# Routing inside the expert pairs of a fused attention and experts kernel: powers made one pair ahead, another order on GpSimd and VectorE, all slots written out

## The reference

```python
# x, ctx: (16, 256, 256); 8 experts, hidden width 704, the two best experts of each token
def attention(q, c, wq, wk, wv):           # q is ctx, c is the normalized x
    Q, K, V = c @ wq, q @ wk, q @ wv
    return softmax(Q @ K.T) @ V
def experts(x, Wg, W1, W2, W3):
    scores = x @ Wg.T
    top_scores, top_idx = top_k(scores, 2)
    y[e] = (silu(x @ W1[e].T) * (x @ W2[e].T)) @ W3[e].T
    return sum(top_scores[k] * y[top_idx[k]] for k in range(2))
x = x + tanh(g_xattn) * attention(ctx, layernorm(x), wq, wk, wv)
x = x + tanh(g_ffn) * experts(layernorm(x), Wg, W1, W2, W3)
```

## Time and profile before

| what | value |
|---|---|
| runs | 657.65, 661.85, 660.46 us, median 660.46 |
| profiled execution | 661.32 us, its span 659.5 us |
| busy TensorE (matmuls) | 589.5 us, 89% |
| busy VectorE, ScalarE, GpSimd | 318.4, 329.6, 269.1 us |
| mean granted TensorE clock | 0.962 |
| chain that ended last | PE 61%, DVE 12%, ACT 10%, issue 8%, POOL 5% |

### The profile page before, as it was taken

One profiled execution on the slowest core, in us unless ns is written; L12 is line 12 of the kernel. 1 busy time (PEld: TensorE's weight loads), 2 busy tenths in 40 slices (PEclk: granted clock), 3 DMA queues, 4 the chain that ended last, 5 costly groups with the idle time before them and its releaser, 6 DMA issues.

```text
span 659.5 us, 15092 instructions
## 1 busy us (share of the span) xinstructions
PE 589.5 (89%) x4765; PEld 511.8 (78%) x4766; DVE 318.4 (48%) x860; ACT 329.6 (50%) x474; POOL 269.1 (41%) x245
## 2 busy tenths in 40 slices
PE   5898989898688967789699999799999999999995
PEld 4787878777567855678598989698989898988783
DVE  2488877797656434456333333243433343343332
ACT  3778787887734243433344444244444444444442
POOL 3155565655513655546133333223233333333322
PEclk9899999999878987899799999899999999999999
DMA  8476666855412322215232323132323232322322
GB/s 254 142 233 188 219 203 220 258 169 165 149 35 85 68 60 68 59 34 138 58 59 43 58 36 52 31 54 43 59 43 59 42 56 39 52 42 43 50 43 25
DMA packets 52372, 61.53 MB, mean 93 GB/s; under 512 B 7632, under 2 KB 46160, under 8 KB 52304
## 3 DMA queue, kind: packets, MB, share of 16 engines
q1 hardware_dynamic: 34656, 38.15, 19.2%
q0 software_dynamic: 13296, 18.23, 16.0%
q10 hardware_dynamic: 4352, 4.20, 1.8%
HBM read 36.90 MB, written 23.66 MB: 92 GB/s over the span
## 4 chain that ended last, share of the span: by engine, by line
PE 61%; DVE 12%; ACT 10%; issue 8%; POOL 5%; DMA 2%; another core or an unknown queue 1%; SPq 0%; POOLq 0%; ACTq 0%; DVEq 0%
PE psum L923 30%; PE psum L963 18%; PE psum L818 4%; PE psum L932 4%; PE psum L943 2%; DMA w_in<-in_W3T 2%; ACT w_hi L715 2%; POOL rows_by_expert L586 2%; DVE w_lo L1072 2%; ACT arena L678 2%; ACT w_hi L687 1%; ACT w_hi L691 1%; DVE w_lo L1065 1%; POOL out L623 1%; PE psum L856 1%
## 5 line engine op out<-in xcount | busy, mean ns | idle before, releaser
L623 POOL DMA_INDIRECT out<-w_in,id_s x71 | 126.8, 1786 | 249.2 <-ACT w_in L767 132.4
L923 PE MATMUL psum<-arena,w_hi 128*128 128x256 f16 x1408 | 217.3, 278 | 5.5 <-issue 4.1
L923 PEld LDWEIGHTS psum<-arena,w_hi 128*128 x1408 | 140.3, 100 | 24.7 <-issue 6.2
L923 PE MATMUL psum<-arena,w_lo 128*128 128x256 f16 x704 | 136.9, 277 | 0.0
L749 ACT ACTIVATE arena<-psum 128x1024 f16<-128x1024 f16 (+1 forms) x39 | 36.9, 947 | 95.3 <-PE psum L943 94.8
L818 PE MATMUL psum<-arena 128*128 128x256 f32 x256 | 66.3, 404 | 19.0 <-ACT arena L701 19.0
L1353 DVE SCALAR_TENSOR_TENSOR arena<-psum,h_unit,arena 128x1280 f32<-128x1280 f32 x32 | 49.6, 1550 | 63.8 <-PE psum L923 63.8
L586 POOL DMA_INDIRECT rows_by_expert<-xn2r,slot_i x64 | 66.3, 1036 | 33.8 <-issue 17.4
L923 PEld LDWEIGHTS psum<-arena,w_lo 128*128 x704 | 70.2, 100 | 9.3
L818 PEld LDWEIGHTS psum<-arena 128*128 128x128 f32 x256 | 47.9, 197 | 28.0 <-ACT arena L701 22.4
L1347 DVE SCALAR_TENSOR_TENSOR arena<-psum,h_unit,arena 64x256 f32<-64x256 f32 x32 | 15.7, 491 | 92.3 <-ACT arena L740 92.2
(11 more groups left out here) (183 smaller groups left out, 906.4 us busy)
## 6 DMA issues: line engine op xcount, KB each, us to landing
xa<-rows_by_expert SPq DMA_DIRECT2D x71, 136.0 KB
w_in<-in_W1T SPq DMA_DIRECT2D x8, 704.0 KB
w_in<-in_W3T SPq DMA_DIRECT2D x8, 640.0 KB
w_in<-in_W2T SPq DMA_DIRECT2D x8, 640.0 KB
arena<-in_ctxT SPq DMA_DIRECT2D x16, 256.0 KB
xa<-in_x SPq DMA_DIRECT2D x16, 256.0 KB, 6.0
out<-xa ACTq DMA_DIRECT2D x16, 256.0 KB
out<-w_in,id_s POOLq DMA_INDIRECT x71, 4.4
```

What stands on the lines that cost most here:

```text
L623: pool.indirect_dma_start(out=out[:, :], out_offset=bass.IndirectOffsetOnAxis(ap=id_s[:, t8:t8 + 1], axis=0), in_=y_s[:, t8 % 4, :], in_of ...
L923: ins = pe.matmul(flat_ps[:, j * N2:(j + 1) * N2], w12[w_part][:, c, bass.ds(e * (2 * H) + j * P, P)], xg_t[:, k, x_part, c, :], start=(q ...
```

## The change

- **Slots.** over_slots writes out all 39 slots; no loop and no register-valued wait is left, on GpSimd neither.
- **GpSimd.** In step i: second add of pair i-2, scatter for the batch of pair i-1, low rows for the batch of pair i, power for the batch of pair i+1, first add of pair i-1. The scatter of batch 9 and the low rows of batch 10 move from ahead of the wait for the stores to behind it.
- **VectorE.** In step i: choose (pair i-1's batch), high_rows (pair i's), mixed, weights, slots, moments of pair i+1's batch, combined, low. The units for the scales (units) are made in step 15; choose of batch 9 comes before the last low weights.
- **TensorE.** The rank product stands behind the 17 matmuls of the output. The rows of pair 0 are turned in the last step, before the values of batch 14. Pair 0 begins before the last low weights are there (it waits for them ahead of its sixth chunk), and the probabilities of batch 15 are turned after four of its chunks.
- **ScalarE.** copy_turned for pair 0 in the last step; the last high weights, silu's first call and copy_probs at the head of step 0; norm_rows ahead of copy_rows, copy_turned and high.
- **SyncE.** Pair 0's load no longer waits for the ninth low rows and the fifth even store; pair 1's does.

The diff, cut (functions that are only moved, and the tests for a written index, are left out):

```diff
...
@@ -398,24 +388,15 @@
             for u in range(n):
                 expert[u] = eng.snap(held[UNROLL - n + u], min_val=0, max_val=E - 1)
-        def over_slots(eng, step, take=lambda i, n: None, planned=lambda: None):
-
-
-            def written(a, b):
-                for i in range(a, b):
-                    step(i, i // 2, i % 4, i % UNROLL, lambda m: 0 <= m < SLOTS)
-            written(-2, 0)
-            take(0, EARLY)
-            written(0, EARLY)
-            planned()
-            with eng.Fori(0, 2) as r:
-                take(UNROLL * r + EARLY, UNROLL)
-                for u in range(UNROLL):
-                    step(UNROLL * r + EARLY + u, UNROLL // 2 * r + (EARLY + u) // 2, u % 4, u, lambda m: True)
-            take(PAIRS - UNROLL, UNROLL)
-            written(PAIRS - UNROLL, PAIRS)
-            take(PAIRS, SINGLES)
-            written(PAIRS, SLOTS + 1)
+        def over_slots(eng, step, take=lambda i, n: None):
+
+
+            for i in range(-2, SLOTS + 1):
+                if i >= 0 and i % UNROLL == 0:
+                    if i == EARLY:
+                        eng.wait_ge(s_map, 2)
+                    take(i, min(UNROLL, SLOTS - i))
+                step(i, i // 2, i % 4, i % UNROLL, lambda m: 0 <= m < SLOTS)
         block = ctx.enter_context(nc.Block())
@@ -482,8 +463,7 @@
             sp.wait_ge(s_map, 1)
             for k in range(2):
                 sp.wait_ge(s_scat[k], 16 * KT * TOP_K * ((COUNTED + 1 - k) // 2))
-                sp.wait_ge(s_x2st[k], 16 * (5 - k))
-            sp.wait_ge(s_xn2, 9)
+                sp.wait_ge(s_x2st[k], 16 * 4)
             pad_at = [sp.alloc_register(f"pad_at_{e}") for e in range(E)]
@@ -504,12 +484,15 @@
             def moe_step(i, j, k4, u, on):
                 k = k4 % 2
-                if isinstance(i, int) and i == EARLY - 2:
+                if i == -1:
+                    sp.wait_ge(s_xn2, 9)
+                    sp.wait_ge(s_x2st[0], 16 * 5)
+                if i == EARLY - 2:
                     pads()
                     all_rows()
                 if on(i + 2):
-                    wait_alone(sp, s_id, i + 1)
+                    at_least(sp, s_id, i + 1)
                     for h, (t, _, _) in enumerate(tiles(i + 2, (k4 + 2) % 4)):
                         at = sp.value_load(row_i[0:1, bass.ds(t, 1)], min_val=0, max_val=E * REGION - P)
                         sp.dma_start(xg[:, k, h, :], xs[bass.ds(at, P), :]).then_inc(s_row[k], 16)
@@ -604,37 +587,35 @@
                     low_rows(AT_STEP[n])
             scatter(IN_STEPS - 2)
             second_deviations(IN_STEPS)
-            scatter(IN_STEPS - 1)
-            low_rows(IN_STEPS)
             for k in range(2):
                 pool.wait_ge(s_x2st[k], 16 * (B // 2))
             pool.wait_ge(s_dummy, 16)
-            def add_rows(i, k4):
-
-                for t, half, t8 in tiles(i, k4):
-                    if t8 % 2 == 0:
-                        if not (isinstance(t, int) and t == 0):
-                            pool.wait_ge(s_add[1], 16 * half)
-                    else:
-                        pool.wait_ge(s_add[0], 16 * half + 16)
-                    wait_alone(pool, s_y_copied, t + 1)
-                    pool.indirect_dma_start(
-                        out=out[:, :], out_offset=bass.IndirectOffsetOnAxis(ap=id_s[:, t8:t8 + 1], axis=0),
-                        in_=y_s[:, t8 % 4, :], in_offset=None, compute_op=ALU.add).then_inc(s_add[t8 % 2], 16)
-            for i in range(EARLY):
-                if i + 1 in AT_PAIR:
+            def add_rows(i, h):
+
+                t, half, t8 = tiles(i, i % 4)[h]
+                if t % 2 == 1:
+                    pool.wait_ge(s_add[0], 16 * half + 16)
+                elif t > 0:
+                    pool.wait_ge(s_add[1], 16 * half)
+                pool.wait_ge(s_y_copied, t + 1)
+                pool.indirect_dma_start(
+                    out=out[:, :], out_offset=bass.IndirectOffsetOnAxis(ap=id_s[:, t8:t8 + 1], axis=0),
+                    in_=y_s[:, t8 % 4, :], in_offset=None, compute_op=ALU.add).then_inc(s_add[t % 2], 16)
+            for i in range(SLOTS + 1):
+                if i >= 2 and pair(i - 2):
+                    add_rows(i - 2, 1)
+                if i == 0:
+                    scatter(IN_STEPS - 1)
+                if i - 1 in AT_PAIR:
+                    scatter(AT_PAIR[i - 1])
+                if i in AT_PAIR:
+                    low_rows(AT_PAIR[i])
+                if i + 1 in AT_PAIR and i >= 0:
                     second_deviations(AT_PAIR[i + 1])
-                    low_rows(AT_PAIR[i + 1])
-                if i in AT_PAIR:
-                    scatter(AT_PAIR[i])
-                add_rows(i, i % 4)
-            with pool.Fori(EARLY // 4, PAIRS // 4) as q:
-                for k4 in range(4):
-                    add_rows(4 * q + k4, k4)
-            for i in range(PAIRS, SLOTS):
-                add_rows(i, i % 4)
+                if i >= 1:
+                    add_rows(i - 1, 0)
         @block.scalar
         def _(act):
...
@@ -709,20 +699,19 @@
                     norm_rows(AT_STEP[n])
                 if live(n - 2):
                     store_rows(n - 2)
+                if n == B - 1:
+                    copy_turned(0, 0)
                 if live(n):
                     act.wait_ge(s_scale, n + 1)
                     act.activation(w12[0][:, :, n * H:(n + 1) * H], w12_in[:, k], ACT.Copy,
                                    scale=w_scale[:, 0:1].bitcast(F32)).then_inc(s_hi12, 1)
                     exponents(n)
-                if n == B - 1:
-                    act.activation(silu_first[:], tanh_g[:], ACT.Silu)
                 if live(n + 1):
                     act.wait_ge(s_t1, n + 2)
                     act.activation(x_t, t1_ps, ACT.Copy).then_inc(s_t1_copied, 1)
-                if live(n) and k == 1:
-                    act.activation(w3[0][:, :, e * D:(e + 1) * D], w3_in[:], ACT.Copy,
-                                   scale=w_scale[:, 1:2].bitcast(F32)).then_inc(s_hi3, 1)
+                if live(n) and k == 1 and n < B - 1:
+                    high3(e)
                 if live(n + 1):
                     squares(n + 1)
...
@@ -762,27 +746,29 @@
                 act.wait_ge(s_y, t + 1)
                 act.wait_ge(s_wsum, i + 1)
-                if not (isinstance(t, int) and t < 4):
+                if t >= 4:
                     act.wait_ge(s_add[t8 % 2], 16 * (half - 1))
                 act.activation(y_s[:, t8 % 4, :], y_ps[t8 % 2], ACT.Copy, scale=wsum[:, t8:t8 + 1]).then_inc(s_y_copied, 1)
             def moe_step(i, j, k4, u, on):
                 k = k4 % 2
-                at = i if isinstance(i, int) else None
+                at = i
                 if at == 0:
+                    high3(E - 1)
+                    act.activation(silu_first[:], tanh_g[:], ACT.Silu)
                     copy_probs(B - 1)
+                    act.wait_ge(s_unit, 1)
                 if on(i):
                     gate(i, u)
                 if on(i - 2) and pair(i - 2):
                     copy_product(i - 2, (k4 - 2) % 4, 1)
                 if at in AT_PAIR:
+                    norm_rows(AT_PAIR[at])
                     copy_rows(AT_PAIR[at], x10_ps)
-                if on(i + 1):
+                if i >= 0 and on(i + 1):
                     copy_turned(i + 1, 1 - k)
                 if on(i) and pair(i):
                     high(i, k)
-                if at in AT_PAIR:
-                    norm_rows(AT_PAIR[at])
                 if at == 0:
                     store_rows(B - 2)
                     store_rows(B - 1)
...
@@ -902,6 +898,9 @@
                     rank(AT_STEP[n - 1])
                 if live(n):
                     weight_sum(n)
+                if n == B - 1:
+                    pe.wait_ge(s_t1_copied, B)
+                    turn_gathered(0, 0, 0)
                 if live(n - 1):
                     values(n - 1)
                 if live(n + 1):
@@ -911,7 +910,6 @@
                     turn(t1_ps, xa[:, x_at(m):x_at(m) + KT, :], KT, KD).then_inc(s_t1, 1)
-            pe.wait_ge(s_lo12, 2 * E)
             pe.wait_ge(s_map, 1)
             def to_hidden(chunks, e, k):
...
@@ -978,18 +965,21 @@
             def moe_step(i, j, k4, u, on):
                 k = k4 % 2
-                at = i if isinstance(i, int) else None
+                at = i
                 if on(i):
                     if at == 0:
-                        turn_probs(B - 1)
+                        pe.wait_ge(s_lo12, 2 * E - 1)
                     at_least(pe, s_silu, i)
                     at_least(pe, s_h5, i if pair(i) else PAIRS)
                     pe.wait_ge(s_xgt, i + 1)
                     if pair(i):
                         if at == 0:
                             to_hidden(range(4), expert[u], k)
+                            turn_probs(B - 1)
                             pe.wait_ge(s_v_copied, B)
```

(37 more changed lines are left out.)

55 lines of the change are left out of this document (24 added, 31 removed).

## The result

The median of the changed kernel is 625.57 us (four runs, 624.49 to 627.23), that of the kernel before 660.87 us. The ratio is 0.948 (0.945 to 0.952). The medians lie 35.3 us apart; 626 was predicted. The profiled execution took 624.49 us, its span is 622.80.

A forecast was written before the change was run, and what follows sets the result against it. GpSimd's queue was taken to bound routed pairs 2 to 5, TensorE the stretch after pair 8. Pair 8's turn at 289.4 plus (341.08 - 5.94) gave span 624.5; 1.8 added, 0.9 off: 625.4, given as 626, range 619 to 638.

The forecast's parts named there:

- The circle of GpSimd: Routed pairs 2 to 5: GpSimd's own queue sets the period, 14.2 us (13.5 to 14.4) against 19.06 before.
- Rival A: GpSimd's adds in the routed pairs: two landings in the circle, period 16.7 us, total 633.5; chance 0.14.
- Pairs 1 to 2: From pair 1's power end to pair 2's, no add due: 10.5 us against 23.3 before.
- The opening: Start to P(1): pair 0 starts earlier, but GpSimd's work now stands behind the store wait; 205.1 against 205.7 us.
- P(1): End of the power (reciprocal root) that routed pair 1 needs: forecast at 205.1 us, bounds 204.4 and 207.5.
- The early start of pair 0: Before pair 0: with its rows turned in the last step, TensorE starts it 5 us earlier, bounds 3 and 6.5.
- the moved wait: GpSimd's wait for the last stores, now ahead of batch 9's scatter: takes back the early start; stores land at 197.3.
- To pair 8: From P(5) to the turn of pair 8's rows, after scatters and plan: 31.2 us, at most 32.2.
- P(5): End of the power that routed pair 5 needs: forecast at 258.2 us, against 286.21 before.
- The slots written out: Loop's turn over pairs 8 to 23: 4.10 us standing and lower-clock matmuls go, 5.94 us off, bounds 0 and 5.94.
- The rank product: TensorE in routed pairs: waits 1 us for VectorE's choice; in the old place 2.9, making the period 15.8.
- Rival D: Routed pairs: the power stays behind the adds, period 19.1 us, total 641; chance 0.03.

The follow-up runs named there:

- e8: Changed kernel with the low rows' subtraction made three times in routed pairs 1 to 5 on GpSimd: 637.30 us, ratio 0.969 to the kernel before.
- e10: Changed kernel with GpSimd's low rows moved ahead of the second add in its step: 625.22 us, ratio 0.948 to the kernel before.
- c_changed_again: The changed kernel itself measured a second time, nothing altered: 626.70 us, ratio 0.951 to the kernel before.
- e7: Changed kernel with pair 0's rows turned and copied after the last attention step, as before: 626.69 us, ratio 0.953 to the kernel before.
- e3: Changed kernel with GpSimd's wait for the last stores moved to right before the first add: 621.74 us, ratio 0.943 to the kernel before.
- e1: Kernel before with only all slots written out, every list in its old order: 656.13 us, ratio 0.9937 to the kernel before.
- e2: Changed kernel with the power of pair i put back in step i, behind the second add: 639.77 us, ratio 0.970 to the kernel before.
- e4: Changed kernel with the rank product put back ahead of the 17 output matmuls: 626.36 us, ratio 0.951 to the kernel before.
- e5: Changed kernel with GpSimd's four scatters put ahead of the second add: 628.88 us, ratio 0.953 to the kernel before.
- e9: e3 plus the last batch's scatters ahead of the second add and the other slots' plan right behind the last slots: 618.77 us, ratio 0.940.

## Why the prediction was right, point by point

**The circle of GpSimd** was read rightly: 14.2 us forecast, 14.60, 14.07 and 14.13 measured, and e8 shows that it is this queue; e10, which takes the low rows out of its way, brings the later periods down to 12.4 and 12.7. The terms held: 4.14 from first to second add, 1.87 to the scatters, 5.0 to 5.5 for them, 1.4 for the low rows (the cheap end, 1.40 of the earlier trace rows), 1.0 for variance and power. Rival A (two landings, 16.7) didn't come: the first add's pause is 0.2 to 0.6 us.

**Pairs 1 to 2** were given 10.5 us, and took 10.46.

**The opening** came out 4.0 us earlier than said: P(1) at 201.13, not 205.1. 2.8 us of it is where the attention steps ended in this execution (c_changed_again: 1.4). The early start of pair 0 gave 6.1 us where I took 5: the first long product starts 6.1 us after the power of batch 10, in before 12.2. I had laid it to the early turn of the rows; by e7 that is 2.7 us of it, and the rest comes with the other orders around step 0. The store landed 4.0 us after its issue as taken (4.1), and GpSimd waited 12.97 us for it. That the moved wait takes back what the early start gives was right in kind: from the power of batch 10 to P(1) only 1.8 us were gained, and e3, which moves the wait, got 6.8 there. I had seen the wait, and costed it; I had not said that it could be had back.

**To pair 8** is the term that was mis-sized the other way, 32.68 us against 31.2, and more was off inside it. GpSimd ends its last scatter 26.88 us after P(5) (281.27), not 23.2: the two groups of scatters took 5.88 and 5.90 us where I had 5.2 and 4.9 (in the first, one of 2.08 us at 260.59 began beside VectorE's low product), and the add-to-add interval, 4.11 in my sum, took 5.43 at 267.96; the small rest lies in the gaps. From the end of that scatter to the load at 283.54 it took only 2.27 us, where I had put the bound of 4.1. So two errors offset each other there, and that is luck. First SyncE's queue, then GpSimd's, in after:

```profile
265.93 5.13 SPq L476 DMA_DIRECT2D rows_by_expert<-zrow  x8
```

```profile
267.96 1.60 POOL L603 DMA_INDIRECT out<-w_in,id_s  x1 [0.17 <-issue]
273.39 1.68 POOL L603 DMA_INDIRECT out<-w_in,id_s  x1 [3.83 <-DMA out<-w_in,id_s]
```

The writes of the pad rows run beside that add and its landing. That they are the cause was not tested; in c_changed_again, with the same writes beside it, the interval is 4.72 us. From the landing of the last scatter (282.74) to the turn, 4.3 us, and from the load's issue 3.53 (3.6 taken), were as read:

```profile
283.54 3.77 SPq L498 DMA_DIRECT2D xa<-rows_by_expert  x4
...
287.07 1.01 PE L857 MATMUL psum<-ident,xa 128*128 128x128 f16 x8 [8.77 <-DMA xa<-rows_by_expert]
```

In before TensorE stood 5.93 us at this place, now 8.77, because its work is done sooner than the rows come. In this profile what follows is slower, too. Here are two stretches behind the turn, the first two lines of after and the others of before (columns as in the stages):

```profile
287.07:291.70 4.63, 4.63 (x26) 3.54 (x27) 1.14 (x2) 2.40 (x2) 0.18 (x1) 0.50 0.45 86
291.70:296.40 4.70, 4.70 (x40) 3.97 (x38) 0.77 (x1) 0.47 (x1) 1.56 (x1) 0.86 0.26 28
```

```profile
318.42:323.00 4.58, 4.58 (x30) 3.59 (x31) 1.09 (x2) 2.67 (x3) 0.00 (x0) 0.59 0.25 65
323.00:327.50 4.50, 4.50 (x44) 4.04 (x42) 0.82 (x1) 0.94 (x3) 1.56 (x1) 1.00 0.24 29
```

The granted clock is 0.50 and then 0.86, where it was 0.59 and then 1.00: 1.2 GHz lasts longer. The 17 matmuls behind the turn take 3.63 us instead of 3.26, the next 36 take 4.63 instead of 3.93, and from the turn to pair 8's long product it is 14.53 instead of 13.46 us. This 1.07 us was missing in my sum. That it is the price of the longer stand doesn't follow, though. In c_changed_again TensorE stands 8.75 us at this place, and then:

```profile
288.46:293.09 4.63, 4.63 (x29) 3.65 (x30) 1.14 (x2) 2.56 (x3) 0.20 (x1) 0.56 0.47 81
293.09:297.79 4.70, 4.70 (x46) 4.22 (x44) 0.77 (x1) 1.14 (x3) 1.56 (x1) 1.00 0.26 28
```

There it is 13.62 us to the long product. Over the eleven profiles in which TensorE stands at this turn it is 13.2 to 14.5 us, in no order with the length of the stand: 5.85 us of it go with 13.50 in e1 and with 14.20 in e10. So this stretch differs by 0.9 us between two executions of the same kernel, with how long 1.2 GHz lasts behind the turn; why it lasts longer in one stays open.

**The slots written out** were worth 5.94 us across the loop's turn in e1 and in after, as forecast. The last stage as a whole gave 5.35: 1.07 went as above, and the end of the kernel, from the last long product on, was 0.52 shorter (12.12 us; 12.1 to 13.9 over the 13 profiles). Both lie within what executions of one kernel differ by. By ratio e1 measured 4.2 us (2.5 to 5.7), which leaves room for a little less.

**The rank product** was the weakest step. I said TensorE would wait 1 us for it in each pair; between P(2) and P(5) of after it waits once, 0.40 us. And the alternative, 15.8 us a period in its old place, was wrong: e4's chain has 13.68. The failing estimate is that TensorE starts its step 3 us after P(i). Its 36 matmuls begin 6.9, 5.0, 3.6 and 3.2 us after P(2) to P(5): it comes late and catches up pair by pair, and only at the end stands where I had put it from the start. I had taken TensorE to go in step with the powers, and it doesn't.

**Rival D's price** was off too. With the power behind the adds I had kept the 19.1 us of before; e2 has 16.4, as the other orders count by themselves. The prediction had the whole gain hang on the place of the power, and about half of it, 14.6 of the 27.2 us between P(1) and P(5), comes with the other orders.

So the total of 626 is right partly by luck, because errors cancel: against the forecast span of 624.5 us, the opening is -4.0 with P(1) to P(2) (1.4 to 2.8 of it is only where the attention steps happened to end), the three periods +0.2, the stretch to pair 8 +1.5 and the last stage +0.6, together -1.7, and the span is 622.8. The mechanism stands on e1, e2, e8 and e10 and not on the total.

## What to carry to other kernels

Write the bound of a stage as a circle through the queues, with one row for each term, and test it by lengthening one term: if the period grows nearly one to one (e8), shorten that queue, and look what is next (here TensorE's 12.66 us, 1.6 below). Look at the other engines' pauses as well: an engine that works off a lateness, as TensorE does here, shows no wait from pair to pair, and the whole wait stands at the next handover. When a wait is moved up so that one engine's work may start early, look at everything that now stands behind it: placed only where it is needed, the wait for the stores gave 4 us more. And a stage that ends in a handover (the plan, the scatters, the first load of pair 8) gives back what the stage before it gained unless that handover moves too, as e10 shows.

## What the runs showed of the hardware

Two engines that meet at SBUF both pay, and much: in e5, beside VectorE's 64x256 product of two inputs, GpSimd's copy of 128x2 took 0.81 us instead of 0.20 and its 128x512 subtraction 1.77 instead of 1.16, and that product itself 2.32 instead of 0.42 (2.32 to 2.40 at four places in e5); beside the 128x1280 product the power on 128x2 took 1.95 instead of 0.72. It can also be VectorE alone that pays. In e9, first GpSimd, then VectorE:

```profile
204.22 1.16 POOL L579 TENSOR_TENSOR xn2r<-arena,xn2r 128x512 f16<-128x512 f32 x1
```

```profile
203.62 3.12 DVE L1363 TENSOR_TENSOR w_in<-arena,w_in 128x1280 f16<-128x1280 f32 x1
```

The product took 3.12 us instead of 1.49, and the subtraction its usual 1.16. And in the scatters of e4 above, GpSimd alone pays: one that begins while the 128x1280 product runs is held until 0.83 to 0.88 us behind its end. The Trainium skill, GPSIMD Engine Reference, Specifications, says that the two share their SBUF interfaces and contend when VectorE has two SBUF inputs; these traces agree, and show that VectorE can lose more by it than GpSimd. An add onto rows in HBM that starts when the former has landed costs 4.1 us from start to start where scatters without such a wait go every 1.3 us. The one loop's turn that TensorE comes to in before costs 4.10 us of standing and 1.84 us of matmuls at the lower clock (0.51 granted in the first 3.30 us behind it), and in e1 and after, with the slots written out, TensorE has no pause between pair 8's turn and the last slots but one of 2.15 us at the end, which before has too.
